# First feature products in column blocks of 250, 500 and 500, interleaved with the node transposes from the third tile on

## The chip, the cores and the metric

The kernel runs on one core of one Trainium2 chip. The metric is the device time of one execution in microseconds. Three timed runs of the kernel before gave 1416.03, 1416.58 and 1417.08 us (median 1416.58). The kernel has one launch; its first stage, about 100 us of it, is the place of this change.

## The reference, cut to what matters

1250 nodes with 768 features are normalised row by row. From the normalised rows `xn` come a graph branch (three attention layers over 20000 edges and self loops), a linear-attention branch and, after their sum, a routed feed-forward part. The change touches only the first product of the graph branch:

```python
xn = _layernorm(x, axis=-1)                      # (1250, 768)
...
x1 = jax.nn.relu(xn @ W_ah + b_ah)               # (1250, 768), the input of all three attention layers
xs = [jax.nn.relu(gat_conv(x1, src, dst, W, a_s, a_d, b)) for W, a_s, a_d, b in ...]
```

## The kernel before

The nodes lie in 10 tiles of 125 rows (`P`, `NT`), the features in 6 blocks of 128 (`KT`). The kernel is written out by hand: each engine has its own program, run in order, and the engines wait for each other by semaphores. So the order in the code is the order on the engine.

The stage `front` does this for each node tile t. SyncE (SP) loads the rows (`x_rows(t)`, two DMAs). VectorE (DVE) takes the statistics of tile t+1 (L334 to L337), then subtracts the rounded part of tile t-1 from the transposed values (`low_part`, L344, two halves), takes the reciprocal of the deviation (L355) and normalises tile t in place (L356). TensorE (PE) turns the tile with six transposes (`turn_x`, L530). ScalarE (ACT) copies the transposed values out of PSUM, rounded, into `xnh` (L466, two halves). After that `xnh` and `xnl` (the rest) hold the tile as two fp32r numbers.

The first feature product needs its weights in the same two parts. SP loads block o of `W_ah` (`hidden_weights(o)`, L254), ACT writes the rounded part (`high_part(o)`, L450), GpSimd (POOL) subtracts it from the raw weights (L321). With them PE computes x1 transposed: product i (`hidden(i)`) takes one block of 128 output features and one block of nodes (the columns), 18 matmuls each: 6 feature blocks times three partial products (L101, L102, L103). There are 3 column blocks (`CH`: 418, 416, 416) times 6 output blocks, so 18 products. ACT adds the bias and applies the relu (`take_x1(i)`, L455).

PE's order is: tiles 0 to 3 turned, product 0, tile 4 turned, product 1, tile 5, and so on to tile 9 behind product 5; then products 6 to 17. A column block can start when its node tiles have both their parts: `XL` says how many halves (8, 14 and 20). After product 13 PE multiplies the turned attention weights (`TURNED`, L570, 8 us), after product 15 it turns the result (L576). The loads of loop bounds into PE's registers start in product `REACHED`. Behind product 17 come the scores (L585), their transposes (L590) and the counting of edges (L627), which needs both.

DVE has other work in this stage: a cast of node numbers after tile 1 (L360), casts of the edge lists after tile 6 (L363 to L370), the reach of each tile (L374 to L389), and the score sums over the weights (L401), which go on while PE computes the products. The count of edges begins with L426 and L429.

Of the kernel before, what the change touches and what calls it, by code (L numbers as in the profile page):

```python
# [31 lines left out]
P = 125  # L32
NT = N // P
D = 768
KT = D // 128
# [32 lines left out]

PROJ = (PAIRS - 1,) + tuple(range(PAIRS - 1))
CH = [(0, 418), (418, 416), (834, 416)]  # L70
DH = 64


# [98 lines left out]
def front(nc, g):  # L172
# [3 lines left out]
    with ExitStack() as ctx:  # L176
# [47 lines left out]
        raw_in = [sem(f"raw_in{i}") for i in range(3)]  # L224
# [9 lines left out]
        var_ready, std_ready = sem("var_ready"), sem("std_ready")  # L234
        block = ctx.enter_context(nc.Block())
        ROWS = 2
        X1 = tuple((c, o) for c in range(len(CH)) for o in range(KT))
        XL = (8, 14, 2 * NT)
        REACHED = 10
        TURNED = 13  # L240
        TURNS = ((6, 0, 4), (7, 4, 4), (6, 8, 2))

# [3 lines left out]
        @block.sync  # L246
        def _(sp):
            def x_rows(t):
                if t >= 6:
                    sp.wait_ge(x_in[t % 6], 32)  # L250
                by_rows(sp, xN[:, t, :], g["x"][t * P:(t + 1) * P, :], x_in[t % 6])

            def hidden_weights(o):
                sp.dma_start(w_raw[o][:, :, :], g["w_ah"][o]).then_inc(raw_in[o % 3], 16)  # L254

            def half_layer(i):
                layer, half = i // 2, i % 2
                if i >= 2:
                    sp.wait_ge(wl_used, i - 1)
                sp.dma_start(wl[half][:, :, :], g["w_gat"][layer, :, half * KT // 2:(half + 1) * KT // 2, :])\  # L260
                    .then_inc(wl_in[half], 16)

            x_rows(0)
            x_rows(1)
            x_rows(2)
            x_rows(3)
            hidden_weights(0)
            x_rows(4)
            hidden_weights(1)
            sp.dma_start(g["bah"][:, :], g["b_ah"]).then_inc(bias_in, 16)  # L270
            x_rows(5)
            hidden_weights(2)
            x_rows(6)
            x_rows(7)
            x_rows(8)
            x_rows(9)
            sp.dma_start(chunk_i[:, :], g["dst_c"]).then_inc(edges_in, 16)
            sp.dma_start(src_i[:, :], g["src_t"]).then_inc(edges_in, 16)
            sp.dma_start(dst_i[:, :], g["dst_t"]).then_inc(edges_in, 16)
            for o in range(3, KT):  # L280
                sp.wait_ge(raw_in[o % 3], 16)
                hidden_weights(o)
            for layer in range(ROWS):
                sp.dma_start(a_bc[layer][:, :, :], g["a_gat"][layer].partition_broadcast(128)).then_inc(a_in, 16)
            half_layer(0)
            half_layer(1)
            sp.wait_ge(ends_ready, 1)
            sp.dma_start(g["dram_ends"].rearrange("e (c u) -> c e u", u=2), ends[:, :, :]).then_inc(ends_in, 16)
            sp.wait_ge(ends_in, 16)
            for k, row in enumerate((lowest_in, highest_in)):  # L290
                sp.dma_start(row[:, :], g["dram_ends"][k].partition_broadcast(NT)).then_inc(ends_in, 16)
            sp.wait_ge(reach_ready, 1)
            sp.dma_start(g["reach_row"][0:1, :], reach[:, :]).then_inc(reach_in, 16)
            sp.wait_ge(xt_full, 2 * NT)
            sp.dma_start(wT[:, :, :], g["w_turned"]).then_inc(wT_in, 16)
            sp.dma_start(a_blk[:, :, :], g["a_block"]).then_inc(wT_in, 16)
            for i in range(2, 2 * ROWS):
                half_layer(i)
            sp.wait_ge(x1_full, 3 * KT)
            sp.dma_start(g["wq_raw"][:, :, :], g["w_qkv"][PAIRS - 1]).then_inc(wq_in, 16)  # L300
            sp.wait_ge(a_low, 2)
            sp.dma_start(g["dram_a"], abT[0:HEADS, :]).then_inc(scores_out, 16)
            sp.dma_start(g["dram_low"], low[:, :]).then_inc(scores_out, 16)
            sp.wait_ge(scores_out, 32)
            sp.wait_ge(bias_in, 16)
# [22 lines left out]
        def _(dve):  # L328
# [63 lines left out]
            for layer in range(ROWS):  # L392
                for k in range(KT):
# [4 lines left out]
                    for s in range(2):  # L398
# [18 lines left out]
                        dve.value_load(g["reach_row"][0:1, 2 * w + 1:2 * w + 2], min_val=1, max_val=ET)) for w in range(NT)]  # L417
            dve.wait_ge(at_ready, len(CH))
            own.done(nc.vector.tensor_reduce(low[:, :], abT[0:HEADS, :], axis=AX.X, op=ALU.min))
# [23 lines left out]
        def _(act):  # L443
# [4 lines left out]
            def high_part(o):  # L448
                act.wait_ge(raw_in[o % 3], 16 * (o // 3 + 1))
                nc.scalar.activation(w_high[o][:, :, :], w_raw[o][:, :, :], ACT.Copy).then_inc(high_ready, 1)  # L450

            def take_x1(i):
                (c0, n), o = CH[X1[i][0]], X1[i][1]
                act.wait_ge(x1_full, i + 1)
                nc.scalar.activation(x1T[:, o, c0:c0 + n], bank(4 + i % 3)[:, 0:n], ACT.Relu,  # L455
                                     bias=g["bah"][:, o:o + 1]).then_inc(x1_free, 1)
# [4 lines left out]
            for t in range(NT):  # L461
                if t + 1 < NT:
                    deviation(t + 1)
                for i in (2 * t, 2 * t + 1):
                    act.wait_ge(xt_full, i + 1)
                    nc.scalar.activation(xnh[:, 3 * (i % 2):3 * (i % 2) + 3, t * P:(t + 1) * P],  # L466
                                         bank(i % 4)[:, 0:3 * P].rearrange("p (k n) -> p k n", k=3), ACT.Copy)\
                        .then_inc(xt_free, 1)
                if 2 <= t < 2 + KT:
                    high_part(t - 2)  # L470
                if t == 4:
                    act.wait_ge(bias_in, 16)
                if t >= 4:
                    take_x1(t - 4)
            for i in range(NT - 4, len(X1)):
                take_x1(i)
                if i == TURNED:
                    act.wait_ge(waT_full, 1)
                    for half in range(2):
                        nc.scalar.activation(waT[:, 384 * half:384 * (half + 1)], bank(half)[0:2 * HL, 0:384], ACT.Copy)\  # L480
                            .then_inc(waT_ready, 1)
                if i == TURNED + 2:
                    act.wait_ge(wa_full, 1)
                    nc.scalar.activation(wa[:, :, :].rearrange("p k (s h) -> p k s h", s=2)[:, :, :, ROWS * HL:HEADS],
                                         bank(2)[:, 0:KT * 2 * HL].rearrange("p (k s h) -> p k s h", k=KT, s=2), ACT.Copy)\
                        .then_inc(wa_ready, 1)
# [35 lines left out]
        def _(pe):  # L522
# [10 lines left out]

            def hidden(i):
                c, o = X1[i]
                c0, n = CH[c]
                if c == 0:
                    pe.wait_ge(low_ready, o + 1)
                if o == 0:
                    pe.wait_ge(xl_ready, XL[c])  # L540
                if i >= 3:
                    pe.wait_ge(x1_free, i - 2)
                for k in range(KT):
                    last = split_matmul(nc, bank(4 + i % 3)[:, 0:n], (w_high[o][:, k, :], w_low[o][:, k, :]),
                                        (xnh[:, k, c0:c0 + n], xnl[:, k, c0:c0 + n]), k == 0, k == KT - 1)
                    if i >= REACHED and k % 2 == 0:
                        load_reach()
                last.then_inc(x1_full, 1)
# [8 lines left out]
                    reached.append(pe.value_load(g["reach_row"][0:1, j:j + 1], min_val=j % 2, max_val=ET - 1 + j % 2))  # L557

            pe.wait_ge(const_ready, 5)
            for t in range(4):  # L560
                turn_x(t)
            for i in range(len(X1)):
                hidden(i)
                if i + 4 < NT:
                    turn_x(i + 4)
                if i == TURNED:
                    pe.wait_ge(wT_in, 32)
                    for half in range(2):
                        for c in range(KT):
                            last = nc.tensor.matmul(bank(half)[0:2 * HL, 0:384], a_blk[:, c, :], wT[:, c, 384 * half:384 * (half + 1)],  # L570
                                                    start=c == 0, stop=c == KT - 1)
                    last.then_inc(waT_full, 1)
                if i == TURNED + 2:
                    pe.wait_ge(waT_ready, 2)
                    for k in range(KT):
                        last = nc.tensor.transpose(bank(2)[:, 2 * HL * k:2 * HL * (k + 1)], waT[:, 128 * k:128 * (k + 1)],  # L576
                                                   ident[0:2 * HL, 0:2 * HL])
                    last.then_inc(wa_full, 1)
# [1317 lines left out]
```

## Time and profile before

| | us |
|---|---|
| median of three runs | 1416.58 |
| profiled execution | 1416.86 |
| its span | 1414.9 |
| PE busy in the span | 1355.7 (96%) |
| DVE busy | 1047.7 (74%) |
| ACT busy | 500.8 (35%) |
| POOL busy | 41.3 (3%) |

The page cuts the span into 40 slices of 35.4 us. PE is at 9 or more tenths in nearly all of them; the first slice has 5 tenths. So the first 35 us are the one long stretch in which PE waits, and they lie in the stage described above. Time of a stage is read from the timeline of its engines, since the shares of the whole span say nothing about it.

### The profile page before, as it was taken

The numbers are of one execution on the slowest core, as the hardware profiler recorded it, in microseconds if no ns is written. First come the engines' busy times: TensorE is split into PE (matmuls) and PEld (weight loads), VectorE is DVE, ScalarE is ACT, GpSimd is POOL, SyncE is SP. The second block draws the span as 40 slices with busy tenths as digits, with TensorE's granted clock in tenths as the row PEclk, the third lists the DMA queues.
The fourth block names the chain that finished last, engine by engine and source line by source line (L and its number), as shares of the span: only waits on it lengthen the run. The fifth ranks groups of instructions, "written<-read, shape, count | busy, mean of one in ns | idle before, by whom it ended". The sixth has DMA issues, their size and how long they took to land.

```text
span 1414.9 us, 21075 instructions
## 1 busy us (share of the span) xinstructions
PE 1355.7 (96%) x8144; PEld 1267.2 (90%) x8144; DVE 1047.7 (74%) x1927; ACT 500.8 (35%) x820; POOL 41.3 (3%) x43
## 2 busy tenths in 40 slices
PE   5999999999999799999999999999999999999897
PEld 4964566999999799999999999999999999999885
DVE  6867988799999842686676677676757766768667
ACT  3211134334334511444333433343243324333373
POOL 3100000000000050000000000000000000000000
PEclk9999999999999899999999999999999999999998
DMA  9310000221221574511101110111012011104003
GB/s 292 104 68 2 0 1 3 87 89 71 89 89 38 180 218 160 138 37 37 39 1 71 37 40 1 70 37 40 1 70 76 1 70 37 42 1 137 7 1 109
DMA packets 23619, 91.59 MB, mean 65 GB/s; under 512 B 3681, under 2 KB 4864, under 8 KB 20589
## 3 DMA queue, kind: packets, MB, share of 16 engines
q1 hardware_dynamic: 22609, 88.07, 19.2%
q10 hardware_dynamic: 924, 2.30, 0.6%
q8 instruction: 62, 1.02, 0.3%
q14 instruction: 24, 0.20, 0.0%
HBM read 79.30 MB, written 11.06 MB: 64 GB/s over the span
## 4 chain that ended last, share of the span: by engine, by line
PE 53%; DVE 6%; ACT 1%; issue 1%; DVEq 0%
PE psum L1699 25%; PE psum L101 8%; PE psum L102 8%; PE psum L103 8%; DVE hN L1323 1%; PE psum L1713 1%; DVE prob L1307 1%; DVE prob L1301 1%; PE psum L1753 1%; DVE acc L1345 0%; DVE x1l L1330 0%; PE psum L1768 0%; ACT prob L1529 0%; DVE acc L1361 0%; DVE xll L1336 0%
## 5 line engine op out<-in xcount | busy, mean ns | idle before, releaser
L1699 PE MATMUL psum<-hN,prob 125*125 125x193 f32 x2400 | 409.0, 327 | 1.5 <-DVE hN L1323 1.5
L1699 PEld LDWEIGHTS psum<-hN,prob 125*125 125x125 f32 x2400 | 395.4, 187 | 2.0 <-issue 1.8
L1529 ACT ACTIVATE prob<-prob,acol 125x1250 f32<-125x1250 f32 x120 | 160.9, 1341 | 381.5 <-DVE prob L1301 381.5
L1307 DVE SCALAR_TENSOR_TENSOR prob<-prob,cnt 125x1250 f32<-125x1250 f32 x120 | 174.7, 1456 | 56.3 <-ACT prob L1529 56.3
L1301 DVE SCALAR_TENSOR_TENSOR prob<-vrow,ncol,urow 125x1250 f32<-125x1250 f32 x120 | 182.0, 1516 | 9.5 <-PE psum L1699 9.5
L742 DVE CUSTOM_DVE_ANT_0 junk<-mask,arow 125x1250 bf16<-125x1250 uint8 x120 | 174.8, 1457 | 3.1
L101 PE MATMUL psum<-woh,xlh 128*125 128x384 f32 x360 | 127.2, 353 | 2.6 <-DVE acc L1345 2.6
L101 PE MATMUL psum<-wph,x1h 128*125 128x384 f32 x330 | 118.4, 359 | 4.8 <-PEq L958 1.9
L102 PE MATMUL psum<-wol,xlh 128*125 128x384 f32 x360 | 122.6, 340 | 0.0
L103 PE MATMUL psum<-woh,xll 128*125 128x384 f32 x360 | 121.9, 339 | 0.0
L103 PE MATMUL psum<-wph,x1l 128*125 128x384 f32 x330 | 111.9, 339 | 0.0
L102 PE MATMUL psum<-wpl,x1h 128*125 128x384 f32 x330 | 111.9, 339 | 0.0
L627 PE MATMUL psum<-hot_src,hot_dst 125*125 125x418 bf16 x540 | 110.5, 355 | 0.8 <-DVE hot_src L429 0.8
L101 PE MATMUL psum<-wq_high,xnh 128*125 128x256 f32 x360 | 103.0, 286 | 1.3 <-PEq L176 1.3
L627 PEld LDWEIGHTS psum<-hot_src,hot_dst 125*125 125x125 bf16 x540 | 60.9, 136 | 47.5 <-DVE hot_src L429 38.8
L102 PE MATMUL psum<-wq_low,xnh 128*125 128x256 f32 x360 | 101.6, 282 | 0.0
L103 PE MATMUL psum<-wq_high,xnl 128*125 128x256 f32 x360 | 101.5, 282 | 0.0
L429 DVE TENSOR_SCALAR hot_src<-node_id,src_f 125x1250 bf16<-125x1250 f16 x180 | 97.7, 543 | 0.0
L1330 DVE TENSOR_TENSOR x1l<-x1T,x1h 128x750 fp32r<-128x750 f32 x54 | 50.8, 941 | 60.0 <-ACT x1h L1537 59.3
L1336 DVE SCALAR_TENSOR_TENSOR xll<-psum,xlh 128x375 fp32r<-128x375 f32 x60 | 32.8, 547 | 80.9 <-ACT xlh L1548 80.9
L1537 ACT ACTIVATE x1h<-x1T 128x750 fp32r<-128x750 f32 x54 | 44.9, 831 | 73.7 <-PE psum L103 73.7
L101 PEld LDWEIGHTS psum<-woh,xlh 128*125 128x125 f32 x360 | 67.2, 187 | 4.1 <-issue 3.9
(241 smaller groups left out, 2216.4 us busy)
## 6 DMA issues: line engine op xcount, KB each, us to landing
arow<-scratch_a SPq DMA_DIRECT2D x12, 625.0 KB, 4.0
urow<-scratch_uv SPq DMA_DIRECT2D x12, 625.0 KB, 4.1
vrow<-scratch_uv SPq DMA_DIRECT2D x12, 625.0 KB, 5.7
wq_raw<-in_w_qkv SPq DMA_DIRECT2D x6, 1152.0 KB, 6.7
wp_raw<-in_w_pair SPq DMA_DIRECT2D x6, 1152.0 KB, 7.5
wo_raw<-in_w_out SPq DMA_DIRECT2D x6, 1152.0 KB, 5.1
wl<-in_w_gat SPq DMA_DIRECT2D x4, 1152.0 KB, 11.0
xN<-in_x SPq DMA_DIRECT2D x10, 336.0 KB
```

The source lines that it names most:

```text
L101: nc.tensor.matmul(psum, s_high, m_high, start=first, stop=False)
L102: nc.tensor.matmul(psum, s_high, m_low, start=False, stop=False)
L103: return nc.tensor.matmul(psum, s_low, m_high, start=False, stop=last)
L429: nc.vector.tensor_scalar(hot_src[:, e, :], node_id[:, :], src_f[:, bass.ds(unit + e, 1)], None, ALU.is_equal).then_inc(hot_ready, 1)
L627: last = nc.tensor.matmul(at_window(w, c)[0:P, 0:n], hot_dst[:, e, 0:P], hot_src[:, e, c0:c0 + n], start=False, stop=False, skip_group_che ...
L742: own.done(nc.vector.tensor_tensor_reduce(out=junk[:, :], in0=mask[:, t, :], in1=arow[head % 2][0:P, :], scale=1.0, scalar=0.0, op0=ALU.mu ...
L1301: nc.vector.scalar_tensor_tensor(prob[n % RING][:, :], vrow[head % 2][0:P, :], ncol[:, head, j:j + 1], urow[head % 2][0:P, :], op0=ALU.add ...
L1307: nc.vector.scalar_tensor_tensor(prob[n % RING][:, :], prob[n % RING][:, :], 1.0, cnt[:, n % NT, :], op0=ALU.min, op1=ALU.mult).then_inc(p ...
L1330: nc.vector.tensor_tensor(low[:, :, :], x1T[:, :, t * P:(t + 1) * P], high[:, :, :].bitcast(F32), ALU.subtract)\
L1529: nc.scalar.activation(prob[n % RING][:, :], prob[n % RING][:, :], ACT.Exp, bias=acol[:, n // NT, n % NT:n % NT + 1]).then_inc(e_ready, 1)
L1537: nc.scalar.activation(x1_parts(i, t)[0][:, :, :], x1T[:, :, t * P:(t + 1) * P], ACT.Copy).then_inc(xh_ready, 1)
L1699: last = nc.tensor.matmul(bank(t // 2)[0:P, 193 * (t % 2):193 * (t % 2) + 193], ring[:, t * P:(t + 1) * P], hN[i % 2][:, j, 193 * s:193 * ...
```

## The change

The 18 products keep their number and their 1250 columns in all, but the column blocks are now 250, 500 and 500 (`XCH`). The other users of `CH` keep 418, 416 and 416. The first block needs two node tiles for its columns, the second six, so `XL` becomes 4, 12, 20. PE turns only tiles 0 and 1 ahead of product 0, and then one tile behind each product, so tile 9 is turned behind product 7. ACT makes the rounded weights of block o already in the turn of tile o (before: of tile o + 2), and takes product t - 2 in the turn of tile t (before t - 4). SP issues the weight loads between the first tiles. `REACHED` goes from 10 to 11.

```diff
+XCH = [(0, 2 * P), (2 * P, 4 * P), (6 * P, 4 * P)]
...
-        X1 = tuple((c, o) for c in range(len(CH)) for o in range(KT))
-        XL = (8, 14, 2 * NT)
-        REACHED = 10
+        X1 = tuple((c, o) for c in range(len(XCH)) for o in range(KT))
+        XL = (4, 12, 2 * NT)
+        REACHED = 11
...
             x_rows(0)
             x_rows(1)
+            hidden_weights(0)
             x_rows(2)
+            hidden_weights(1)
             x_rows(3)
-            hidden_weights(0)
+            sp.dma_start(g["bah"][:, :], g["b_ah"]).then_inc(bias_in, 16)
+            hidden_weights(2)
             x_rows(4)
-            hidden_weights(1)
-            sp.dma_start(g["bah"][:, :], g["b_ah"]).then_inc(bias_in, 16)
             x_rows(5)
-            hidden_weights(2)
-            x_rows(6)
-            x_rows(7)
-            x_rows(8)
-            x_rows(9)
+            for o in range(3, KT):
+                sp.wait_ge(raw_in[o % 3], 16)
+                hidden_weights(o)
+                x_rows(o + 3)
+            x_rows(NT - 1)
...
-            for o in range(3, KT):
-                sp.wait_ge(raw_in[o % 3], 16)
-                hidden_weights(o)
...
-                if 2 <= t < 2 + KT:
-                    high_part(t - 2)
-                if t == 4:
+                if t < KT:
+                    high_part(t)
+                if t == 2:
                     act.wait_ge(bias_in, 16)
-                if t >= 4:
-                    take_x1(t - 4)
-            for i in range(NT - 4, len(X1)):
+                if t >= 2:
+                    take_x1(t - 2)
+            for i in range(NT - 2, len(X1)):
...
-            for t in range(4):
+            for t in range(2):
                 turn_x(t)
             for i in range(len(X1)):
                 hidden(i)
-                if i + 4 < NT:
-                    turn_x(i + 4)
+                if i + 2 < NT:
+                    turn_x(i + 2)
```

ACT's program behind its first two deviations, before. `xnh` is the copy of a turned tile, `wah_high_83` to `_85` are the rounded weights of output blocks 0 to 2, `std` is the deviation of the next tile:

```order
L466 ACTIVATE xnh<-psum 128x3x125 x2
L446 ACTIVATE std<-moments,eps 125x1
L466 ACTIVATE xnh<-psum 128x3x125 x2
L446 ACTIVATE std<-moments,eps 125x1
L466 ACTIVATE xnh<-psum 128x3x125 x2
L450 ACTIVATE wah_high_83<-wah_raw_89 128x768
L446 ACTIVATE std<-moments,eps 125x1
```

And now (the line numbers of the changed kernel are off by one):

```order
L465 ACTIVATE xnh<-psum 128x3x125 x2
L449 ACTIVATE wah_high_83<-wah_raw_89 128x768
L445 ACTIVATE std<-moments,eps 125x1
L465 ACTIVATE xnh<-psum 128x3x125 x2
L449 ACTIVATE wah_high_84<-wah_raw_90 128x768
L445 ACTIVATE std<-moments,eps 125x1
L465 ACTIVATE xnh<-psum 128x3x125 x2
```

The rounded weights of block 0 now stand behind the copy of tile 0, ahead of the deviation of tile 2, and so POOL's subtraction of block 0, which waits for them, falls beside DVE's work on tile 1. DVE's and POOL's own orders are the same as before.

SP's issues behind the first two tiles, before. `xN` with 112 and 13 rows is one node tile, `wah_raw` one block of weights:

```order
L94 DMA xN<-in_x 112x768
L95 DMA xN<-in_x 13x768
L94 DMA xN<-in_x 112x768
L95 DMA xN<-in_x 13x768
L254 DMA wah_raw_89<-in_w_ah 128x768
L94 DMA xN<-in_x 112x768
```

And now:

```order
L255 DMA wah_raw_89<-in_w_ah 128x768
L95 DMA xN<-in_x 112x768
L96 DMA xN<-in_x 13x768
L255 DMA wah_raw_90<-in_w_ah 128x768
L95 DMA xN<-in_x 112x768
L96 DMA xN<-in_x 13x768
```

The first two weight blocks each went ahead of a node tile, so tile 2 is one load and tile 3 two loads later in the queue; the edge lists are last, behind all six weight blocks.

## Rows read from the trace of the kernel before

**Rows 1.** Timeline of PE: start, length (us), engine, line, what, count, idle before

```profile
18.88 1.51 PE L530 MATMUL psum<-ident,xN 125*128 125x125 f32 x6 [1.95 <-DVE xN L356]
21.64 0.69 PE L101 MATMUL psum<-xnh,wah_high 128*128 128x418 f32 x1 [1.25 <-DVE xnl L344]
...
27.76 0.80 PE L530 MATMUL psum<-ident,xN 125*128 125x125 f32 x6
...
36.85 0.86 PE L530 MATMUL psum<-ident,xN 125*128 125x125 f32 x6 [0.28 <-DVE xN L356]
...
41.56 0.86 PE L530 MATMUL psum<-ident,xN 125*128 125x125 f32 x6 [0.44 <-DVE xN L356]
...
50.26 0.80 PE L530 MATMUL psum<-ident,xN 125*128 125x125 f32 x6
50.82 0.43 PE L101 MATMUL psum<-xnh,wah_high 128*128 128x416 f32 x1
...
101.43 12.77 PE L585 MATMUL psum<-x1T,wa 128*24 128x418 f32 x36 [0.70 <-ACT x1T L455]
```

**Rows 2.** Timeline of ACT in the same stretch

```profile
9.22 1.11 ACT L466 ACTIVATE xnh<-psum 128x375 fp32r<-128x375 f32 x2 [1.45 <-PE psum L530]
...
28.28 0.86 ACT L466 ACTIVATE xnh<-psum 128x375 fp32r<-128x375 f32 x2 [6.46 <-PE psum L530]
29.03 0.85 ACT L450 ACTIVATE wah_high<-wah_raw 128x768 fp32r<-128x768 f32 x1
...
61.36 0.61 ACT L455 ACTIVATE x1T<-psum,bah 128x416 f32<-128x416 f32 x1 [2.81 <-PE psum L103]
64.78 0.61 ACT L455 ACTIVATE x1T<-psum,bah 128x416 f32<-128x416 f32 x1 [2.81 <-PE psum L103]
```

**Rows 3.** Timeline of DVE in the same stretch

```profile
11.02 0.68 DVE L356 TENSOR_SCALAR xN<-xN,moments,rstd 125x768 f32<-125x768 f32 x1
11.62 0.81 DVE L360 CAST node_id<-node_i 125x1250 f16<-125x1250 int32 x1
...
13.64 0.95 DVE L344 TENSOR_TENSOR xnl<-psum,xnh 128x375 fp32r<-128x375 f32 x2
...
18.15 0.68 DVE L356 TENSOR_SCALAR xN<-xN,moments,rstd 125x768 f32<-125x768 f32 x1
...
29.91 2.30 DVE L356 TENSOR_SCALAR xN<-xN,moments,rstd 125x768 f32<-125x768 f32 x1
...
34.48 2.31 DVE L356 TENSOR_SCALAR xN<-xN,moments,rstd 125x768 f32<-125x768 f32 x1
```

**Rows 4.** Timeline of POOL in the same stretch

```profile
18.28 2.22 POOL L321 TENSOR_TENSOR wah_low<-wah_raw,wah_high 128x768 fp32r<-128x768 f32 x1 [12.80 <-ACT wah_high L450]
...
29.95 1.84 POOL L321 TENSOR_TENSOR wah_low<-wah_raw,wah_high 128x768 fp32r<-128x768 f32 x1 [5.99 <-ACT wah_high L450]
34.51 1.86 POOL L321 TENSOR_TENSOR wah_low<-wah_raw,wah_high 128x768 fp32r<-128x768 f32 x1 [2.72 <-ACT wah_high L450]
```

**Rows 5.** Timeline of DVE, the first statistics of tiles 0 and 1

```profile
4.71 0.56 DVE L334 BATCH_NORM_STATS2 stats<-xN 125x6 f32<-125x384 f32 x1 [3.83 <-DMA xN<-in_x]
...
6.18 0.56 DVE L334 BATCH_NORM_STATS2 stats<-xN 125x6 f32<-125x384 f32 x1 [0.20 <-DMA xN<-in_x]
```

**Rows 6.** Timeline of PE in the attention stage, matmuls of 256 columns

```profile
249.87 0.28 PE L102 MATMUL psum<-wq_low,xnh 128*125 128x256 f32 x1
249.99 0.28 PE L103 MATMUL psum<-wq_high,xnl 128*125 128x256 f32 x1
```

**Rows 7.** Timeline of DVE where the scores come in

```profile
114.77 1.44 DVE L419 TENSOR_REDUCE low_a<-abT 12x1 f32<-12x1250 f32 x1 [20.63 <-ACT abT L489]
```

**Rows 8.** Timeline of PE near the end of the kernel

```profile
1370.56 0.54 PE L1779 MATMUL psum<-ident,comb 125*128 125x125 f32 x3 [1.66 <-DVE comb L1418]
...
1374.56 0.53 PE L101 MATMUL psum<-woh,xlh 128*125 128x384 f32 x1
1374.88 0.53 PE L102 MATMUL psum<-wol,xlh 128*125 128x384 f32 x1
```

More of the change, by code:

```diff
@@ L452, in take_x1 @@
             def take_x1(i):
-                (c0, n), o = CH[X1[i][0]], X1[i][1]
+                (c0, n), o = XCH[X1[i][0]], X1[i][1]
                 act.wait_ge(x1_full, i + 1)
@@ L535, in hidden @@
                 c, o = X1[i]
-                c0, n = CH[c]
+                c0, n = XCH[c]
                 if c == 0:
```

## The prediction

> **What bounds the kernel now.** I read the page first: PE is busy 96% of the span, and its 40 slices show the first as the only half-empty one, so a change of the first stage can give at most what PE waits there. Then the timelines of the four engines over the first 55 us, one engine at a time. Three things are to be seen.
>
> First, PE starts its first product at 21.64 us [rows 1], held by DVE, which has to normalise four tiles, one every 3.6 us (11.02 to 18.15 for two, [rows 3]). From 50.82 us on it never waits until 101.43, when the scores begin [rows 1].
>
> Second, between 27.76 and 41.56 PE is not the only bound. Tiles 4, 6 and 7 are turned at 27.76, 36.85 and 41.56, so one every 4.55 and then 4.71 us, and ahead of the last two PE idles 0.28 and 0.44 us for the normalised tile [rows 1]. Yet a product of 416 columns takes 3.42 us (61.36 to 64.78, [rows 2]) and a turn some 0.6 us. So DVE's loop has a pace of its own, 4.55 us.
>
> Third, why that pace: the normalisation takes 0.68 us at 11.02 and 18.15, but 2.30 and 2.31 at 29.91 and 34.48 [rows 3]. In both slow cases POOL's subtraction of a weight block starts 0.04 and 0.03 us behind it (29.95, 34.51) and runs 1.84 to 1.86 us; at 18.15 POOL comes 0.13 us behind it, and there POOL is the one stretched, to 2.22 us [rows 4]. The two can't run at once, and it costs the tile 1.62 us. Both are released by the same event, ACT's copy of a turned tile: copy at 28.28, rounded weights at 29.03, POOL at 29.95 [rows 2, 4]; DVE's `low_part` and reciprocal, then 29.91 [rows 3]. Their race is built into the loop.
>
> **The change, part by part.** It moves no work away: 18 products, 1250 columns times 6. By proportion a product of 500 columns takes 3.42 x 500/416 = 4.11 us and one of 250 takes 2.06. The nearest row for a short one is 0.12 us between two matmuls of 256 columns (249.87, 249.99, [rows 6]), so 18 x 0.12 = 2.16 at most. Taking the 500 from the slope between those and the 416 gives 4.08. Six of each: 6 x (2.06 + 4.11 + 4.11) = 61.7 against 18 x 3.42 = 61.6 before. What changes is when PE starts and what it waits for meanwhile.
>
> *From product 6 to the scores.* Before: 101.43 - 50.82 = 50.6 us. After: the same, plus 12 x (4.11 - 3.42) = 8.3 for the wider products, plus two turns (tiles 8 and 9) that now stand behind products 6 and 7, at 50.82 - 50.26 = 0.56 each, so 1.1, plus some 0.1 for ACT's last, wider copy: 60.1 us. DVE has 4.7 us per tile there and isn't waited for. So the change pays only if product 6 starts before 101.43 - 60.1 = 41.3 us.
>
> *When product 0 starts.* It needs tiles 0 and 1. Their low parts end at 13.64 + 0.95 = 14.6 before [rows 3]. Three edits bear on that. The loads: DVE gets tiles 0 and 1 at 4.71 and 6.18 [rows 5], 1.47 us for one load; a weight block is of about the same size (384 KB against 375). Block 0 is now third in the queue, so it lands near 7.7, ahead of its use at 10.2. Tile 3 is sixth, 6.2 + 4 x 1.47 = 12.1, still ahead of its statistics. DVE's work on earlier tiles covers it, so I cost the loads at nothing; each load later than that would cost 1.5 us. ACT: the copy of tile 0 is at 9.22 and takes 1.1, rounded weights from 10.2, POOL from 10.2 + 0.92 = 11.15 to 13.4. The normalisation of tile 1 at 11.02 is 0.13 us ahead, as at 18.15, and passes. But behind it stands the cast at 11.62, 0.81 us [rows 3], of the same one-input kind. No row shows a cast beside POOL. Bounds: nothing, or the 1.62 us of a normalisation. I take the upper one as the nearest row, less what the race leaves, 1.5. So product 0 starts at 14.6 + 1.5 + 0.1 = 16.2 (bounds 14.7 and 16.4), 5.4 us earlier than before. That is the gain, all of it.
>
> *Products 0 to 5.* PE begins slow: product 0 before took 27.76 - 21.64 = 6.12 us against 3.43 later, which is TensorE at 1.2 instead of 2.4 GHz. 250 columns then take 3.7: tile 2 is turned at 19.9. A slow turn takes 1.51 (18.88, [rows 1]) and keeps PE some 1.4: product 1 at 21.3, of 2.1 to 3.7 us, by when the clock rises; I take 2.9. Tile 3 is turned at 24.2. From here the loop is the one seen before: turn, copy, race, normalise, turn. PE's share of it is 2.1 + 0.6 = 2.7 us, so it waits for DVE, as it did before for 0.28. The length of the product drops out. Tiles 4, 5 and 6 come 4.55 apart, each with a POOL subtraction beside it (blocks 3 to 5; the order of both engines against the copy is unchanged); tile 7 comes 4.71 after tile 6, the casts of the edge lists being in it (36.85 to 41.56, [rows 1]). Tile 7 is turned at 24.2 + 3 x 4.55 + 4.71 = 42.6, product 6 starts at 43.2. That is 1.9 us later than break-even.
>
> Sum: the start gives -5.4; from product 0 to product 6 it is 43.2 - 16.2 = 27.0 us against 50.82 - 21.64 = 29.2, so -2.2, though six products there lost 40% of their columns; and what they lost is paid behind, 60.1 against 50.6, +9.5. That is +1.9 us, the scores at 103.3 instead of 101.4.
>
> *Behind it.* DVE is through with its score sums at 114.77 - 20.63 = 94.1 [rows 7], and PE asks for them at 101.4. They come 2 us later, as tile 9 is turned near 52 instead of 50.26, and stay hidden. The edge lists are now behind all 16 loads, near 6.2 + 14 x 1.47 = 26.8, and are used near 38. The register loads move by one product, PE doesn't wait for them. All after the scores shifts rigidly.
>
> On the race, the Trainium skill (SBUF — State Buffer, "Who interferes with whom") says that VectorE in a mode with two ports and GpSimd hold a shared pair of ports exclusively, and that whoever issues first keeps it for the whole instruction. The trace agrees on the exclusion (2.30 against 0.68) but not on the winner at 29.91, where DVE's row starts first by 0.04 and is the stretched one [rows 3, 4]. By the rule as written the sum would be that of the first rival below; by the rows it is the one above.
>
> **The rivals.**
>
> *No collision* (the other side, faster). If the normalisation wins its race, as at 18.15, three tiles cost 1.62 us less each: product 6 at 43.2 - 4.9 = 38.3, the scores at 98.4, 3.0 us earlier than before: 1413.6. For it: the margin is some hundredths of a microsecond, and 0.13 decides the other way. Against it: both warm cases in the rows lost, with equal margins, and the releasing chain is the same. It decides as soon as two of the three tiles pass.
>
> *The slow clock.* In the new loop PE has 2.1 us of product and then 2.5 us of transposes and idling. Near the end of the kernel, after nine transposes with 1.66 us of idling between them, matmuls of 384 columns came 0.32 us apart (1374.56, 1374.88, [rows 8]): half speed. If that happens here, the loop becomes PE's, 3.7 + 1.4 = 5.1 us a tile, +0.55 each over three or four, and product 6 starts slow, which costs up to the 6.12 - 3.43 = 2.7 us that product 0 cost before. With parts of both, +3.5 on top: 1422. For it: the like stretch in rows 8. Against it: the pause there was somewhat longer, and PE's products at 27.76 to 41.56 stayed fast with turns and short waits between them. [...]
>
> *DVE's score sums become late.* The score sums end at 96 against scores at 103: it would take 7 us more, and only then cost anything. I give it next to nothing.
>
> **How the numbers follow.** Profiled execution 1416.86 (span 1414.9) + 1.9 = 1418.8; that execution lies 0.3 above the median of 1416.58, so the median becomes 1418.5. Chances: the forecast 0.48, slow clock 0.30, no collision 0.22. A change counts from 0.2%, 2.8 us, about what can be told here. The forecast's own range is 1416.8 to 1420.3 (cast free: -1.5; clock late in product 1 and a third collision at tile 3: +1.7), and a fifth of it lies over 1419.4. Slower: 0.10 + nearly all of 0.30 = 0.38. Faster: about three quarters of 0.22 = 0.17. Same: 0.45. The range takes in most of both rivals: 1413.6 to 1423.
>
> **What would show it.** Right: first product of 250 columns near 16.2; turns of tiles 4 to 6 at distances of 4.5 us with PE idle 1.5 us or more before each, and normalisations of 2.3 us; the cast of node numbers over 2 us; product 6 near 43; the scores near 103. Wrong: normalisations of 0.68 us throughout (then faster), 250-column matmuls 0.21 us apart in products 3 to 5 (then slower), or a tile whose statistics wait for its load.

## The result, and the profile after

| | before | changed | |
|---|---|---|---|
| median of the runs, us | 1416.53 (12 runs) | 1419.65 (12 runs) | ratio 1.002, 95% interval 1.0013 to 1.0027 |
| span of the profiled execution, us | 1414.9 | 1419.6 | |

The changed kernel is 3.1 us slower, by the median. The runs of before lie between 1415.45 and 1418.58, those of the changed one between 1417.22 and 1421.61; the section on the changed kernel's second profile comes back to that width. Of the changed kernel's twelve, the six with a mean granted clock of 0.987 took 1420.0 to 1421.6 us and the six with 0.988 to 0.992 took 1417.2 to 1419.3; the profiled one is the slowest of all.

The stage, cut at the same four events in both traces, with the rows of the busy times between them. First the kernel before: up to product 0, up to product 6, up to the scores, up to the first counting matmul, and to the end of the first counting (columns: stretch, length, busy us and instructions by engine, granted clock of PE, share of the DMA engines, GB/s).

```profile
0.00:21.64 21.64, 6.02 (x24) 4.52 (x25) 15.10 (x38) 8.03 (x18) 6.79 (x13) 1.00 0.95 246
21.64:50.82 29.18, 27.88 (x144) 25.95 (x145) 20.30 (x40) 10.79 (x26) 9.65 (x5) 1.00 0.49 174
50.82:101.43 50.61, 49.91 (x250) 42.85 (x248) 39.12 (x207) 9.58 (x18) 0.00 (x0) 1.00 0.27 95
101.43:117.51 16.08, 14.71 (x49) 5.09 (x49) 2.46 (x5) 2.94 (x5) 0.89 (x2) 1.00 0.21 74
117.51:150.97 33.46, 33.46 (x162) 17.92 (x163) 33.46 (x109) 2.27 (x2) 0.32 (x1) 1.00 0.01 2
```

The same cuts in the changed kernel:

```profile
0.00:16.81 16.81, 3.00 (x13) 2.28 (x13) 10.13 (x24) 5.83 (x12) 6.51 (x14) 1.00 0.92 235
16.81:44.55 27.74, 19.73 (x145) 18.74 (x145) 25.03 (x45) 10.10 (x25) 8.93 (x5) 1.00 0.79 233
44.55:104.55 60.00, 59.23 (x262) 44.12 (x260) 43.07 (x217) 11.94 (x23) 0.00 (x0) 1.00 0.24 80
104.55:120.64 16.09, 14.72 (x50) 5.09 (x50) 2.46 (x5) 2.94 (x5) 0.90 (x2) 1.00 0.21 74
120.64:155.26 34.62, 34.62 (x162) 19.16 (x163) 33.77 (x109) 2.26 (x2) 0.31 (x1) 0.95 0.01 2
```

The lengths differ by -4.83, -1.44, +9.39, +0.01 and +1.16 us; the remaining 1264 us by +0.4. That is the +4.7 of the spans. Up to the scores it is +3.12. In the second row PE is busy 19.73 of 27.74 us, against 27.88 of 29.18 before: that is the waiting that the forecast spoke of. The last row is another thing: the granted clock is 0.95 there and was 1.00. That column does not show the slow beginning: it says 1.00 in the second row too, though the matmuls of 250 columns come 0.21 us apart up to 20.78 us and 0.12 after 21.77.

The turns of tiles 3 to 7 on PE in the changed kernel, against [rows 1]:

```profile
25.62 0.86 PE L529 MATMUL psum<-ident,xN 125*128 125x125 f32 x6 [1.53 <-DVE xN L355]
...
30.15 0.86 PE L529 MATMUL psum<-ident,xN 125*128 125x125 f32 x6 [1.57 <-DVE xN L355]
...
34.68 0.86 PE L529 MATMUL psum<-ident,xN 125*128 125x125 f32 x6 [1.57 <-DVE xN L355]
...
39.21 0.86 PE L529 MATMUL psum<-ident,xN 125*128 125x125 f32 x6 [1.56 <-DVE xN L355]
...
43.93 0.86 PE L529 MATMUL psum<-ident,xN 125*128 125x125 f32 x6 [1.76 <-DVE xN L355]
```

The tiles come 4.53 us apart, and 4.72 at the last, nearly as they did with products of 418 columns (4.51 to 4.58, and 4.71); PE only waits longer before each, 1.5 to 1.8 us for 0.28 to 0.44. And the reason is where it was in [rows 3, 4], DVE's normalisation:

```profile
11.96 1.81 DVE L355 TENSOR_SCALAR xN<-xN,moments,rstd 125x768 f32<-125x768 f32 x1
13.69 0.80 DVE L359 CAST node_id<-node_i 125x1250 f16<-125x1250 int32 x1
...
23.27 2.30 DVE L355 TENSOR_SCALAR xN<-xN,moments,rstd 125x768 f32<-125x768 f32 x1
...
27.83 2.27 DVE L355 TENSOR_SCALAR xN<-xN,moments,rstd 125x768 f32<-125x768 f32 x1
```

beside POOL's subtractions:

```profile
11.55 1.80 POOL L320 TENSOR_TENSOR wah_low<-wah_raw,wah_high 128x768 fp32r<-128x768 f32 x1 [6.08 <-ACT wah_high L449]
...
23.34 1.81 POOL L320 TENSOR_TENSOR wah_low<-wah_raw,wah_high 128x768 fp32r<-128x768 f32 x1 [4.85 <-ACT wah_high L449]
27.86 1.81 POOL L320 TENSOR_TENSOR wah_low<-wah_raw,wah_high 128x768 fp32r<-128x768 f32 x1 [2.72 <-ACT wah_high L449]
```

POOL starts 0.07 and 0.03 us behind the normalisations at 23.27 and 27.83, and stretches both to 2.3 us.

### The profile page after: what moved, and what is told of

Same layout as the page of the kernel before. It is cut to its first block, busy times and chain, and to the rows that moved or that the text cites. A ratio compares the mean times of both kernels' runs of the same rounds, so it can differ in the third digit from the quotient of the medians.

```text
span 1419.6 us, 21075 instructions
## 1 busy us (share of the span) xinstructions
PE 1355.2 (95%) x8144; PEld 1260.5 (89%) x8144; DVE 1051.5 (74%) x1927; ACT 500.0 (35%) x820; POOL 40.2 (3%) x43
## 4 chain that ended last, share of the span: by engine, by line
PE 53%; DVE 6%; ACT 1%; issue 1%; DVEq 0%
PE psum L1698 25%; PE psum L102 8%; PE psum L103 8%; PE psum L104 8%; DVE hN L1322 1%; PE psum L1712 1%; DVE prob L1306 1%; DVE prob L1300 1%; PE psum L1752 1%; DVE acc L1344 0%; PE psum L1767 0%; DVE x1l L1329 0%; ACT prob L1528 0%; DVE acc L1360 0%; DVE xll L1335 0%
```

## The experiments

Theory: POOL's subtraction of a weight block, released by the same copy as DVE's normalisation, stretches it and sets a pace of 4.5 us a tile, so narrower first products save PE's time only to have it wait, and the wider ones behind them are paid in full. Rivals: the pace is that of the chain itself; the loads; TensorE's slow clock.

### The collision taken out of the changed kernel

```diff
                 if t + 1 < NT:
                     deviation(t + 1)
+                if t < KT:
+                    high_part(t)
                 for i in (2 * t, 2 * t + 1):
                     act.wait_ge(xt_full, i + 1)
                     ...
-                if t < KT:
-                    high_part(t)
```

> The changed kernel with one edit on ACT: the rounded weights of block t are made ahead of the copy of turned tile t, in ACT's idle time while PE turns the tile, and not behind it. POOL's subtraction then starts some 2 us sooner than now and is done before the next normalisation is due. Collision theory: normalisations take 0.68 us, tiles 3 to 6 are turned some 3 us apart instead of 4.53, product 6 starts near 37.5 instead of 44.55 us, the kernel takes some 6 to 7 us less than the changed one, 3 to 4 us less than before (ratio 0.997 to 0.998). Rival, the pace of the loop is that of copy, low parts and statistics and the stretched normalisation only fills time that is idle anyway: tiles stay over 4.2 us apart and the time is that of the changed kernel within 1 us (ratio 1.002). Rival, slow clock: with tiles 3 us apart nothing for it; if matmuls of 250 columns in products 3 to 5 come 0.21 us apart, it is at work.

Measured: 1414.14 us, ratio to before 0.9986 (0.9977 to 0.9995), so 2.7 us faster than before and 3.5 to 5 faster than the changed kernel (ratios 1.0011 and 1.002 in its two comparisons, neither of them beside this kernel). That is less than the 6 to 7 and 3 to 4 expected; the scores are 6.5 us ahead of the changed kernel's first profile, but 4.6 ahead of its second, and the granted clock fell behind the scores here too (last section). DVE and POOL in this kernel, tiles 3 to 5:

```profile
23.01 0.68 DVE L355 TENSOR_SCALAR xN<-xN,moments,rstd 125x768 f32<-125x768 f32 x1
...
26.15 0.68 DVE L355 TENSOR_SCALAR xN<-xN,moments,rstd 125x768 f32<-125x768 f32 x1
...
29.09 0.68 DVE L355 TENSOR_SCALAR xN<-xN,moments,rstd 125x768 f32<-125x768 f32 x1
```

```profile
23.68 1.83 POOL L320 TENSOR_TENSOR wah_low<-wah_raw,wah_high 128x768 fp32r<-128x768 f32 x1 [4.98 <-ACT wah_high L449]
26.73 1.84 POOL L320 TENSOR_TENSOR wah_low<-wah_raw,wah_high 128x768 fp32r<-128x768 f32 x1 [1.22 <-ACT wah_high L449]
```

POOL now begins 0.6 us behind, the normalisations take 0.68, tiles 4 to 6 are turned 2.9 us apart, and the scores begin at 98.10 (104.55 in the changed kernel). So the rival, that the pace is that of the chain itself, is out. Product 6 begins at 38.10. The work done on POOL is the same; only its place moved, by the order of two instructions on ACT.

### The same edit on the kernel before

```diff
+                if 2 <= t < 2 + KT:
+                    high_part(t - 2)
                 for i in (2 * t, 2 * t + 1):
                     ...
-                if 2 <= t < 2 + KT:
-                    high_part(t - 2)
```

> The kernel before with the same edit: the rounded weights of block t-2 are made ahead of the copy of turned tile t. Collision theory: PE becomes the bound of products 0 to 5 (3.43 us and a turn of 0.6), tiles 4 to 9 are turned 4.1 us apart instead of 4.51 to 4.71, so the stage and the kernel take some 2 us less than before (ratio 0.9985). Together with the same edit on the changed kernel it tells what the interleaving is worth when nothing collides: some 1.5 us. Rival, the stretched normalisation fills idle time: no difference, ratio 1.000.

Measured: 1415.22 us, ratio 0.9989 (0.998 to 0.9998): 1.6 us faster. Its tiles 4 to 6 are turned at 27.20, 31.28 and 35.36, 4.08 us apart as PE's product and turn want it, and the scores begin at 99.78. Tile 7 comes 5.03 us behind tile 6, not 4.1: a subtraction now meets a cast of the edge lists, which takes 1.76 us instead of 0.24, and PE idles 0.81. All normalisations take 0.68 us in both kernels, and the interleaved kernel's scores are 1.7 us ahead of the other's. But each still has one cast that collides (in the interleaved one that of the node numbers, 2.42 us), so 1.7 is not the worth of the interleaving without any collision. By the runs the difference is 1.1 us, and the two intervals overlap, so that the traces show it and the times alone would not.

### The column blocks alone

```diff
+XCH = [(0, 2 * P), (2 * P, 4 * P), (6 * P, 4 * P)]
...
-        XL = (8, 14, 2 * NT)
+        XL = (8, 12, 2 * NT)
...
-                (c0, n), o = CH[X1[i][0]], X1[i][1]
+                (c0, n), o = XCH[X1[i][0]], X1[i][1]
```

(and the same in `hidden`; four tiles are still turned first, and the loads are those of before)

> The kernel before with the new column blocks of 250, 500 and 500 alone: four tiles turned ahead of product 0, loads and ACT's order as before. My reading is that the length of products 1 to 5 drops out of the loop, since DVE and POOL set its pace. Then product 0 starts at 21.6 as before, ends at 25.3, and tiles 4 to 7 are still 4.5 to 4.7 us apart; tiles 8 and 9 too (4.5, and 3 without a subtraction beside it). Product 6 starts near 47, and the 12 wide products give 49.3 + 8 + 1: the scores come near 106, 4.5 to 5 us later than before (ratio 1.003). Rival, PE's columns count: the total of columns is the same, so the scores come within 1 us of before, ratio 1.000.

Measured: 1421.42 us, ratio 1.0035 (1.0022 to 1.0048), 4.6 us slower. PE in this kernel:

```profile
22.37 0.55 PE L102 MATMUL psum<-xnh,wah_high 128*128 128x250 f32 x1 [1.25 <-DVE xnl L345]
...
31.14 0.86 PE L531 MATMUL psum<-ident,xN 125*128 125x125 f32 x6 [1.57 <-DVE xN L357]
...
35.68 0.86 PE L531 MATMUL psum<-ident,xN 125*128 125x125 f32 x6 [1.58 <-DVE xN L357]
```

The same total of columns, and PE idles 1.57 and 1.58 us before tiles 5 and 6 (1.76 and 1.58 before 7 and 8). Product 0 begins 0.7 us later than before, product 6 at 48.49 and the scores at 107.12, the last two 1.5 and 1.1 us behind what was expected. The length of a product drops out where another engine has the pace, and it is paid where PE has it. So of the change, the blocks cost about 4.6 us (five runs), and by subtraction the earlier start gave 1.5 to 2.8 of it back.

### The loads of before

SP's loads in the order of the kernel before, all else as in the changed kernel (the diff is the SP part of the change, turned round).

> The changed kernel with SP's loads in the order of before (four tiles, weight block 0, and so on). In the changed kernel tile 1 reaches DVE at 6.58 us instead of 6.18 and tile 2 at 9.72 us, when DVE already waits for it. Loads theory: with the old order the first two come back to 4.7 and 6.2, tile 1 is turned about 1 us sooner if weight block 0 (which then lands near 10.8) does not hold up ACT; product 0 starts near 16.3 instead of 16.81 and all is 0.3 to 0.8 us faster than the changed kernel. Rival: the weights late, POOL's first subtraction at 11.7 instead of 11.55 and product 0 unmoved or later: no difference within 0.5 us. Either way the loads are a small part of the 3.1 us.

Measured: 1420.93 us, ratio 1.0027 (1.0017 to 1.0036), no faster than the changed kernel, where 0.3 to 0.8 us had been expected. Product 0 begins at 16.75 us (16.81), the scores at 104.33 (104.55). Tile 1 still reached DVE at 6.58 us, so the order of the loads is not what holds it there. It was indeed turned sooner, at 12.15 for 13.83, but then POOL caught the cast behind its normalisation:

```profile
11.42 0.68 DVE L357 TENSOR_SCALAR xN<-xN,moments,rstd 125x768 f32<-125x768 f32 x1
12.02 2.42 DVE L361 CAST node_id<-node_i 125x1250 f16<-125x1250 int32 x1
```

2.42 us instead of 0.81: here is the price that no row of before showed. Early or late, one of the two instructions meets POOL's first subtraction (11.96 us here, 11.55 in the changed kernel), and product 0 waits for it.

### The weights a little later

```diff
                 if t >= 2:
                     take_x1(t - 2)
+                if t < KT:
+                    high_part(t)
```

(and taken out ahead of it)

> The changed kernel with the rounded weights made behind the take of the product, so some 0.35 us later from tile 2 on; tiles 0 and 1 are as in the changed kernel. Race theory: what matters is only which of the two begins first by some tenths of a microsecond. Here the normalisation begins 0.4 us ahead, takes 0.68 us, and POOL is stretched to 2.1 to 2.2. The weights then are late by 0.6 us, which paces two tiles at 7.0 us: tiles 3 to 7 at 3.5 us, product 6 near 40, scores near 100, 4 to 5 us faster than the changed kernel. Rival: POOL's work takes its time from DVE wherever it falls, so the later start stretches statistics or low parts instead and the tiles stay 4.5 us apart.

Measured: 1416.31 us, ratio 0.9998 (0.9988 to 1.0007), 2.1 us faster than the changed kernel beside it (1418.42, the last experiment), not 4 to 5. The race part held: normalisations of tiles 3 to 6 take 0.68 us, POOL 1.96 to 1.97, beginning 0.39 to 0.40 us behind. The casts of the edge lists now met a subtraction (the first took 1.92 us for 0.28) and tile 7 came 5.42 us behind tile 6; still, product 6 began at 40.01, as expected. The scores came at 101.53, not near 100, and that is the slow clock. The rest of the miss lies in the measure: the 4 to 5 us were reckoned from scores at 104.55, and the changed kernel's came at 102.66 in this comparison. PE around product 6:

```profile
39.39 0.86 PE L529 MATMUL psum<-ident,xN 125*128 125x125 f32 x6 [2.30 <-DVE xN L355]
40.01 0.47 PE L102 MATMUL psum<-xnh,wah_high 128*128 128x500 f32 x1
40.32 0.53 PE L103 MATMUL psum<-xnl,wah_high 128*128 128x500 f32 x1
40.65 0.62 PE L104 MATMUL psum<-xnh,wah_low 128*128 128x500 f32 x1
41.07 0.62 PE L102 MATMUL psum<-xnh,wah_high 128*128 128x500 f32 x1
...
44.15 0.39 PE L104 MATMUL psum<-xnh,wah_low 128*128 128x500 f32 x1
44.38 0.39 PE L102 MATMUL psum<-xnh,wah_high 128*128 128x500 f32 x1
```

with the granted clock of the stretch beside it:

```profile
40.00:45.00 5.00, 5.00 (x18) 4.08 (x17) 2.21 (x6) 1.37 (x4) 0.00 (x0) 0.66 0.06 3
45.00:50.00 5.00, 5.00 (x26) 4.22 (x26) 1.75 (x4) 1.43 (x3) 0.00 (x0) 1.00 0.00 0
```

Matmuls of 500 columns come 0.42 us apart (1.2 GHz) and then 0.23 (2.4 GHz). The granted clock is 0.66 there. Product 6 takes 5.73 us instead of 4.21, so the fall costs 1.5 us. Ahead of it PE had idled 2.30 us and then made transposes. It is one profile; whether the fall comes in every execution was not tried.

### Two casts moved as well

To the first experiment's kernel:

```diff
                 if t >= 1:
                     low_part(2 * t - 2)
                     low_part(2 * t - 1)
+                if t == 2:
+                    dve.wait_ge(const_ready, 5)
+                    own.done(nc.vector.tensor_copy(node_id[:, :], node_i[:, :]))
...
-                if t == 1:
-                    dve.wait_ge(const_ready, 5)
-                    own.done(nc.vector.tensor_copy(node_id[:, :], node_i[:, :]))
-                if t == 6:
+                if t == 7:
                     dve.wait_ge(edges_in, 48)
```

> The changed kernel with the rounded weights ahead of the copy, and two casts of DVE moved: that of the node numbers from behind tile 1's normalisation to ahead of tile 2's, where DVE waits for a slow product anyway, those of the edge lists from tile 6 to tile 7, where PE has products of 500 columns. Theory, DVE's chain is the bound up to product 6 and nothing behind it: product 0 near 15.0 instead of 16.4, tile 7 turned 2.95 instead of 4.71 us behind tile 6, product 6 near 35, scores near 95, 3 us less than without the two moves and 6.5 less than before (ratio 0.9955). Rival: the reach and the score sums come too late and PE waits ahead of the scores, with a gain under 1 us from the moves.

Measured: 1410.39 us, ratio 0.9956 (0.9943 to 0.997). The tiles 6 and 7, which the edge lists had kept 4.7 us apart, and the scores:

```profile
32.17 0.86 PE L529 MATMUL psum<-ident,xN 125*128 125x125 f32 x6
...
35.11 0.86 PE L529 MATMUL psum<-ident,xN 125*128 125x125 f32 x6
...
95.72 12.77 PE L584 MATMUL psum<-x1T,wa 128*24 128x418 f32 x36 [0.77 <-ACT x1T L454]
```

Product 0 begins at 15.71, product 6 near 35.7, the scores at 95.72, 5.7 us ahead of before; the time is 6.2 us less, and 8.0 less than the changed kernel's in the same comparison. At the scores the two moves gave 2.4 us (98.10 to 95.72), where 3 had been expected; product 0 came at 15.71, not 15.0. So a kernel with these column blocks and this interleaving is faster than the kernel before, once DVE's chain is short. How much of that is the interleaving's is not shown: the kernel before with both of these edits, the early weights and the moved casts, was not run.

### A middle form

Three tiles first, `XCH = [(0, 374), (374, 438), (812, 438)]`, `XL = (6, 14, 20)`; the casts ahead of tile 3's normalisation and behind tile 8's; all else like the kernel above.

> A middle form: three tiles turned ahead of product 0, column blocks of 374, 438 and 438, the rounded weights ahead of the copy, the casts of node numbers ahead of tile 3's normalisation, those of the edges behind tile 8's. A product of 374 columns and a turn take 3.7 us, more than DVE's 2.95, so PE never waits after it has begun. Product 0 near 18.2, product 6 near 42.6, scores near 96: 5.4 us less than before (ratio 0.996), 1 us more than with two tiles ahead. If instead DVE needs more than 3.7 us a tile, it ends near that of the changed kernel with early weights (0.9985).

Measured: 1411.93 us, ratio 0.9966 (0.9952 to 0.9979). Product 0 begins at 19.22 (a microsecond late, as tile 2 waited 1.87 us for its load), tiles 3 to 8 are turned 3.74 us apart with PE never idle, product 6 begins at 43.52 and the scores at 96.94, each about a microsecond later than expected. It is no better than two tiles first, by 1.2 us in the traces; by the runs the two can't be told apart.

### The changed kernel again

> The changed kernel again, beside the kernel before and the others on one chip. Ratio 1.002 to 1.0025 as measured. In its profile the scores come near 104.5 again. Open is the stretch from 117 to 125 us, where PE's granted clock was 0.79 and the first counting cost 1.2 us more than in the kernel before: if it is tied to the schedule, it is seen again; if it is chance, the clock is 1.00 there and the span 1 us shorter.

Measured: 1418.42 us, ratio 1.0011 (1.0002 to 1.002), span 1416.1, so 1.8 us slower than before, and a smaller ratio than the 1.002 expected. Here the scores begin at 102.66, not at 104.55. The reason is mostly tile 3. DVE and POOL in this profile:

```profile
23.01 0.68 DVE L355 TENSOR_SCALAR xN<-xN,moments,rstd 125x768 f32<-125x768 f32 x1
...
25.95 2.31 DVE L355 TENSOR_SCALAR xN<-xN,moments,rstd 125x768 f32<-125x768 f32 x1
```

```profile
23.13 2.25 POOL L320 TENSOR_TENSOR wah_low<-wah_raw,wah_high 128x768 fp32r<-128x768 f32 x1 [5.07 <-ACT wah_high L449]
26.00 1.85 POOL L320 TENSOR_TENSOR wah_low<-wah_raw,wah_high 128x768 fp32r<-128x768 f32 x1 [0.62 <-ACT wah_high L449]
```

Tile 2 was still turned slowly (its six transposes took 1.45 us, 1.23 in the first profile) and ACT's copy of it took 1.11 us instead of 0.89. Counted from the start of that copy, POOL's subtraction begins 0.22 us later than in the first profile and DVE's normalisation 0.17 us later. So POOL's start is 0.12 us behind DVE's instead of 0.07, and DVE passes. And from 117 to 125 us the clock stayed at 1.00, where the first profile had 0.79. The kernel is the same, so both differ from one execution to the next: 1.4 us at tile 3 and 1.2 us at the first counting; another 0.4 is product 0's start (16.38 for 16.81). Together that is 3.0 us, against a spread of 4.4 us between the first comparison's runs.

## Why the prediction was right, point by point

**The start.** Forecast product 0 at 16.2, 5.4 us earlier; measured 16.81 and 16.38 in the two profiles. Against the 14.6 + 0.1 us of before, the 1.5 us came out as 2.1 and 1.7. That is near, but partly by luck: they are made of other parts than forecast. I had the whole of it fall on the cast of node numbers, and I costed the loads at nothing because they land in turn, 1.47 us each. In the changed kernel tile 2 reached DVE at 9.72 and 9.98 us, not at 9.1, when DVE had idled 1.13 and 1.82 us for it:

```profile
9.72 0.56 DVE L333 BATCH_NORM_STATS2 stats<-xN 125x6 f32<-125x384 f32 x1 [1.13 <-DMA xN<-in_x]
```

```profile
9.98 0.56 DVE L333 BATCH_NORM_STATS2 stats<-xN 125x6 f32<-125x384 f32 x1 [1.82 <-DMA xN<-in_x]
```

Tile 1's normalisation stands behind those statistics and began at 11.96 and 12.21, 0.9 and 1.2 us later than the 11.02 of before. POOL, 0.41 and 1.09 us ahead of it, then stretched it by 1.13 and 0.45 us, and the cast took its usual 0.80. So the cast of over 2 us, one of my signs for the forecast, did not come, and a tile that waits for its load, one of those against it, did. Why tile 2 is later than in turn was not tried; the same order of loads brought it at 8.81 in the first experiment's profile.

The two parts trade places. With the loads of before, and in the first experiment's kernel, tile 1's normalisation begins at 11.42 and 11.05, the cast is stretched to 2.42 us in both, and product 0 begins at 16.75 and 16.38. So the late load cost nothing in the end, but not for the reason that I gave.

**Products 0 to 5.** Forecast 27.0 us, measured 27.74. The loop of 4.55 and 4.71 us came as 4.53 and 4.72. The term that was too small is tile 3, turned at 25.62 for 24.2: the third collision, which I had only in the range. The clock rose sooner than I took it to: product 1 already has its matmuls 0.12 us apart. The second profile, where tile 3 passes, has product 6 at 42.7 (forecast 43.2).

**Product 6 to the scores.** Forecast 60.1, measured 60.0 in the first profile and 59.95 in the second.

**Sum.** Forecast +1.9 at the scores; +3.12 and +1.23 in the two profiles, whose mean is 2.2. The runs of the first comparison say +3.1, those of the second +1.8. What the forecast left out was the clock behind the scores: in the first profile counting starts with PE at half speed and loses 1.16 us. I had said that all behind the scores shifts rigidly, and that failed. The range was also added up a little wide: its own terms, 1418.5 - 1.5 and + 1.7, give 1417.0 to 1420.2, not 1416.8 to 1420.3. The forecast's direction stands, and its range holds the median in both comparisons; +3.1 lies just past the 2.8 us from which the forecast counts a change, +1.8 well short of it.

**No collision.** It was not what happened, but its price was right: made on purpose by the first experiment, it gave 2.7 us less than before, where I had 3.0, with the scores at 98.10 (98.4). The rule that break-even lies at product 6 near 41.3 us fits all profiles with these blocks, interleaving and a full clock: from product 6 to the scores they take 59.9 to 60.0 us, whether product 6 begins at 35.73, 38.10, 42.71 or 44.55.

**The slow clock.** Not in products 3 to 5 of the changed kernel: matmuls of 250 columns stay 0.12 us apart, though PE is idle or transposing for about half of the time. In the kernel with the weights a little later it fell once, at the beginning of product 6, at a price of 1.5 us, within the 2.7 I gave. There PE had idled 2.30 us, against the 1.5 to 1.8 ahead of the changed kernel's products. So the rival's price is real, but the loop for which I had feared it did not bring it on in either profile.

**The score sums** stayed hidden: in the changed kernel DVE is through with them at 97.4 us (117.90 less 20.52 of idling), 7 us before PE asks for them.

## What to carry to other kernels

Before narrowing one engine's pieces to start it sooner, ask who sets the pace while it runs them; where it is another engine, the narrow pieces save nothing and the wide ones behind them are paid in full (4.6 us here). Where two engines that exclude each other are released by one event, their order can be decided by hundredths of a microsecond, and then comes out alike in nearly every round; move the one with slack into a stretch where the other has nothing to do, as one swap of two instructions on a third engine did here (3.5 to 5 us). A normalisation that takes 0.68 us in one row and 2.3 in the next deserves a look even where no long wait stands beside it.

## What the runs showed of the hardware

DVE's normalisation (0.68 us alone), its casts (0.24 to 0.81) and POOL's subtraction (1.80 to 1.86) did not get on side by side in any profile. In the kernel before, the pair begun at 18.15 us ended at 20.50, and that begun at 29.91 ended at 32.21: 2.3 to 2.4 us, near the 2.5 of the two one after the other. Where POOL's row began up to 0.07 us behind DVE's, or ahead of it and not within 0.11 us of its end, DVE was the one stretched (normalisations to between 1.13 and 2.31 us, casts to between 1.76 and 2.42). Where it began 0.12 to 0.5 us behind a normalisation or the cast of node numbers, POOL was, to between 1.96 and 2.25. Nothing between 0.07 and 0.12 was seen. So the first start in a trace doesn't tell who wins. DVE's statistics (0.54 to 0.56) and low parts (0.95 to 1.00 with PE at full speed), which ran beside the same subtractions, kept their times.

The clock of TensorE fell at the start of counting in four of the ten profiles. Over the 6 us from the first counting matmul the granted clock was 0.72 in the changed kernel, 0.72 with the collision taken out, 0.77 with the column blocks alone and 0.73 with the loads of before; it was 1.00 in the kernel before, in the changed kernel's second profile and in the other four. The same program had it once and once not. What stands in front is the same in all: the scores, ten small transposes, three products of 418 columns and two short waits. That the fall takes 0.9 to 1.2 us is shown by the length of the first counting; what decides it was not tried and stays open.
